# Row tails of a graph kernel stored in 28 parts, and three moves in the order of ScalarE, VectorE and TensorE

## The reference

```python
h  = relu(layernorm(x))
agg = segment_sum(relu(h[src]), dst)                       # layer 0
x1 = x + relu(relu((h + agg) @ W1 + b1) @ W2 + b2)
h  = relu(layernorm(x1))                                   # layer 1
deg_inv = where(deg > 0, deg ** -0.5, 0)                   # deg: edges per dst
norm = deg_inv[src] * deg_inv[dst] * edge_weight
Q, K, V = relu(h @ Wq + bq), h @ Wk + bk, h @ Wv + bv      # 8 heads of 8
hidden = V * hopwise[0]
hop 0:    Kj = relu(K[src] + edge_attr);  M = segment_sum(norm * outer(Kj, V[src]), dst)
hops 1,2: M = segment_sum(norm * M[src], dst)
each hop: H = Q . M;  hidden += hopwise[hop + 1] * H / max(1, |H| / sqrt(8))
out = x1 + hidden
```

## Time and profile before

| | us |
|---|---|
| median of 3 runs | 1816.73 (1809.44 to 1824.96) |
| profiled execution | 1815.59 |
| its span, first to last instruction | 1812.7 |
| DVE busy | 1488.8 (82%) |
| PE busy | 1345.3 (74%) |
| POOL busy | 1193.0 (66%) |
| ACT busy | 1015.2 (56%) |
| mean granted TensorE clock | 0.86 of full |

### The profile page before, as it was taken

How to read it: one execution, slowest core, us unless ns; L and a number is a source line. 1 busy time by engine, 2 the same in 40 slices (tenths; PEclk the granted TensorE clock), 3 DMA queues, 4 the chain that set the end, 5 groups by cost and what they waited for, 6 DMA issues and landing times. The chain is left out here.

```text
span 1812.7 us, 22165 instructions
## 1 busy us (share of the span) xinstructions
PE 1345.3 (74%) x5794; PEld 840.3 (46%) x5794; DVE 1488.8 (82%) x3207; ACT 1015.2 (56%) x2815; POOL 1193.0 (66%) x1185
## 2 busy tenths in 40 slices
PE   3666778788888985777777277778577898877772
PEld 3455666665666664454544033333233344455551
DVE  5866777789989886799999799999456788699992
ACT  4556878768878875455554255555355556333330
POOL 7775666616665531777773577777477777777776
PEclk9787898879978877798998589888799999988886
DMA  4394333334655554699998588888435554466650
GB/s 126 77 51 123 102 104 102 91 94 132 149 134 141 133 135 92 213 323 319 320 318 293 177 288 305 307 309 299 152 98 159 146 160 135 128 174 175 173 152 17
DMA packets 280787, 313.83 MB, mean 173 GB/s; under 512 B 168577, under 2 KB 198137, under 8 KB 268118
## 3 DMA queue, kind: packets, MB, share of 16 engines
q1 hardware_dynamic: 223734, 246.39, 45.3%
q0 software_dynamic: 56928, 66.04, 14.6%
HBM read 214.54 MB, written 161.32 MB: 207 GB/s over the span
## 5 line engine op out<-in xcount | busy, mean ns | idle before, releaser
L924 PE MATMUL bank<-product,ident 128*128 128x512 f32 (+1 forms) x800 | 383.3, 637 | 134.9 <-DVE product L1278 134.9
L533 POOL DMA_INDIRECT state<-state_hop,slot_of_src x392 | 395.6, 1009 | 126.1 <-issue 108.5
L703 ACT ACTIVATE bank<-state,norm 128x512 f32<-128x512 f32 x392 | 251.1, 679 | 254.9 <-DMA state<-state_hop,slot_of_src 221.6
L1278 DVE TENSOR_TENSOR product<-bank,queries 128x512 f32<-128x512 f32 x392 | 261.2, 687 | 90.0 <-ACT bank L703 88.3
L924 PEld LDWEIGHTS bank<-product,ident 128*128 128x128 f32 x800 | 160.9, 206 | 356.0 <-issue 182.7
L495 POOL DMA_INDIRECT x_edges<-in_x,dst_tiles x196 | 199.5, 1018 | 156.9 <-DVE x_edges L1188 97.0
L509 POOL DMA_INDIRECT row_of_src<-node_rows,pos_int x196 | 195.2, 996 | 122.2 <-DMA node_rows<-row_new 62.8
L495 POOL DMA_INDIRECT x_edges<-in_x,src_tiles x196 | 203.1, 1036 | 95.8 <-issue 54.4
L549 POOL DMA_INDIRECT out<-rows,dst_out x196 | 193.1, 985 | 59.7 <-issue 50.0
L831 PE MATMUL bank<-dst_steps,from_here 128*128 128x197 f32 x392 | 98.6, 406 | 101.7 <-ACT row_no L645 75.2
L1276 DVE SCALAR_TENSOR_TENSOR acc<-acc,same_as_before,bank 128x512 f32<-128x512 f32 x196 | 145.2, 741 | 15.9 <-ACT bank L703 15.1
(11 more groups left out here) (220 smaller groups left out, 3033.0 us busy)
## 6 DMA issues: line engine op xcount, KB each, us to landing
state_hop<-acc SPq DMA_DIRECT2D x98, 1024.0 KB, 4.7
x_nodes<-in_x SPq DMA_DIRECT2D x49, 256.0 KB, 3.6
src_row<-in_src_row SPq DMA_DIRECT2D x49, 256.0 KB, 3.6
out<-out_rows SPq DMA_DIRECT2D x49, 256.0 KB
dst_row<-in_dst_row SPq DMA_DIRECT2D x49, 256.0 KB, 4.5
kv_rows<-kv SPq DMA_DIRECT2D x49, 256.0 KB, 3.5
gg<-head_sums SPq DMA_DIRECT2D x98, 128.0 KB
kv_back<-kv_rows SPq DMA_DIRECT2D x49, 256.0 KB
```

What stands on the lines that cost most here:

```text
L533: pool.indirect_dma_start(out=mg[u % 4][:, k, :], out_offset=None, in_=d_m[hop - 1], in_offset=bass.IndirectOffsetOnAxis(ap=sidx[:, t:t + ...
L703: act.activation(pw[t % len(pw)][:, :], mg[u % 4][:, k, :], ACT.Copy, scale=wn12[:, t:t + 1]).then_inc(weighted, 1)
L924: ins = ten.matmul(ph[:, 0:k * D].rearrange("p (c j) -> p c j", j=HD), ident[:, :], part, start=(r == 0), stop=(r == HD - 1))
L1278: vec.tensor_tensor(ihj(pr[m % 2][:, u % 2 * EH + k, :]), ihj(pw[t % len(pw)][:, :]), over_j(Q[:, t, :]), ALU.mult).then_inc(multiplied, 1)
```

## The change

The store of the row tails is cut into 28 DMAs of 7 columns, at ticks 12 to 39, and POOL waits for all of them. On ACT, the root of the tick's statistics and the signs of the search move from behind the squares of x1 to ahead of the normalised rows, the root first; the signs take the search of group g-3 in place of g-2. On PE, the search moves behind the dense products. On DVE, x1 of the nodes (L1176) moves from the end of the tick to ahead of the statistics, the four comparisons of the selection become one instruction behind the statistics, and the computation of the slots from the signs comes a tick later.

```diff
@@ -61,6 +61,8 @@
 END = max(F_STEP)
 DENSE_TICKS = [2 * k for k in range(1, DU + 1)]
 assert len(DENSE_TICKS) == DU and all(t % 2 == 0 for t in DENSE_TICKS)
+TAIL = 7
+TAIL_AT = {12 + i: i * TAIL for i in range(T // TAIL)}
 DENSE_AT = {t: m for m, t in enumerate(DENSE_TICKS)}
 
 
@@ -405,9 +407,10 @@
                 u = g + 2 - S0
                 if 0 <= u < AU:
                     load_drow(u)
-                if g == 12:
+                if g in TAIL_AT:
+                    c = slice(TAIL_AT[g], TAIL_AT[g] + TAIL)
                     sync.wait_ge(tail_set, 2)
-                    sync.dma_start(by_slot(d_tab)[:, :, D:TW], tail[:, :, :]).then_inc(tail_kept, 16)
+                    sync.dma_start(by_slot(d_tab)[:, c, D:TW], tail[:, c, :]).then_inc(tail_kept, 16)
                 if g == B0 + 3:
                     sync.wait_ge(normed_e, AU)
                     for c in range(2):
@@ -498,7 +501,7 @@
                         bounds_check=top, oob_is_err=False).then_inc(edge_in[e % RI], 16)
 
             pool.wait_ge(pos_set, 1)
-            pool.wait_ge(tail_kept, 16)
+            pool.wait_ge(tail_kept, 16 * len(TAIL_AT))
             for b in range(3):
                 pool.wait_ge(t_kept[b], landed(AU - 1, b, 3))
             for u in range(CU):
@@ -599,6 +602,21 @@
                     act.wait_ge(ends_done, AU)
                     act.activation(flT[:, :], pfl[0:D, 0:2 * TILES], ACT.Copy).then_inc(ends_out, 1)
 
+                if g in STAT_NO:
+                    lo, hi = stats_at(g)
+                    act.wait_ge(varred, STAT_NO[g] + 1)
+                    act.activation(q[:, 3, lo:hi], q[:, 2, lo:hi], ACT.Sqrt, bias=epsc[:, 0:1],
+                                   scale=1.0 / (D * D)).then_inc(rooted, 1)
+                u = g - 3
+                if 0 <= u < CU:
+                    act.wait_ge(searched, u + 1)
+                    for k in range(EH):
+                        t = u * EH + k
+                        each = pair[:, 256 * k:256 * k + T]
+                        act.activation(each, each, ACT.Sign, bias=spm[:, t:t + 1],
+                                       scale=-1.0, accum_out=signs[:, t:t + 1])
+                    act.activation(rowno[:, u * EH:(u + 1) * EH],
+                                   pair[:, :].rearrange("p (k c) -> p k c", c=256)[:, :, T], ACT.Copy).then_inc(counted, 1)
                 if g - 1 in STAT_NO:
                     act.wait_ge(scaled, STAT_NO[g - 1] + 1)
                 u = g - 10 - B0
@@ -634,21 +652,6 @@
                     act.activation(flr[:, :, :], pfl[0:HALF, 0:4 * D].rearrange("p (k f) -> p k f", f=D),
                                    ACT.Copy).then_inc(ends_out, 1)
 
-                u = g - 2
-                if 0 <= u < CU:
-                    act.wait_ge(searched, u + 1)
-                    for k in range(EH):
-                        t = u * EH + k
-                        each = pair[:, 256 * k:256 * k + T]
-                        act.activation(each, each, ACT.Sign, bias=spm[:, t:t + 1],
-                                       scale=-1.0, accum_out=signs[:, t:t + 1])
-                    act.activation(rowno[:, u * EH:(u + 1) * EH],
-                                   pair[:, :].rearrange("p (k c) -> p k c", c=256)[:, :, T], ACT.Copy).then_inc(counted, 1)
-                if g in STAT_NO:
-                    lo, hi = stats_at(g)
-                    act.wait_ge(varred, STAT_NO[g] + 1)
-                    act.activation(q[:, 3, lo:hi], q[:, 2, lo:hi], ACT.Sqrt, bias=epsc[:, 0:1],
-                                   scale=1.0 / (D * D)).then_inc(rooted, 1)
                 if g == 7:
                     act.wait_ge(prep_v, 3)
                     act.activation(tmp2[:, :], tmp[:, :], ACT.Sqrt).then_inc(prep_a, 1)
@@ -823,14 +826,6 @@
                                 ins = ten.matmul(pfl[0:HALF, k * D:(k + 1) * D], lhs, flr[:, 2 * (1 - w) + i, :],
                                                  start=(i == 0), stop=(i == 1), skip_group_check=True)
                     ins.then_inc(fixes, 1)
-                u = g - 2
-                if 0 <= u < CU:
-                    ten.wait_ge(g_set, u + 1)
-                    wait(ten, counted, u)
-                    for k in range(EH):
-                        ins = ten.matmul(pair[:, 256 * k:256 * k + T + 1], gsel[u % 2][:, k * P:(k + 1) * P], delta[:, :],
-                                         start=True, stop=True, skip_group_check=True)
-                    ins.then_inc(searched, 1)
                 if g == B0 + 3:
 
                     ten.wait_ge(ends_out, 1)
@@ -856,6 +851,14 @@
                     ten.wait_ge(relued_d, m + 1)
                     wait(ten, x1_d, m)
                     rows_out(pbd, a1d, W2, 0, HT // 2, mm2_d)
+                u = g - 2
+                if 0 <= u < CU:
+                    ten.wait_ge(g_set, u + 1)
+                    wait(ten, counted, u)
+                    for k in range(EH):
+                        ins = ten.matmul(pair[:, 256 * k:256 * k + T + 1], gsel[u % 2][:, k * P:(k + 1) * P], delta[:, :],
+                                         start=True, stop=True, skip_group_check=True)
+                    ins.then_inc(searched, 1)
                 m = DENSE_AT.get(g - 6)
                 if m is not None:
                     ten.wait_ge(h1_d, m + 1)
@@ -1097,34 +1100,13 @@
 
             for g in range(END + 1):
                 qp, q = st[(g - 1) % RS], st[g % RS]
-                n_sel = 0
-
-                def select(n):
-
-                    nonlocal n_sel
-                    u = g - S0
-                    if 0 <= u < AU:
-                        if n_sel == 0:
-                            vec.wait_ge(drow_in[u % 3], landed(u, u % 3, 3))
-                            wait(vec, turned_e, u - 1)
-                        for k in range(n_sel, n_sel + n):
-                            t = u * EH + k
-                            ins = vec.tensor_scalar(sel[u % 2][:, k * P:(k + 1) * P], drow[u % 3][:, k * P:(k + 1) * P],
-                                                    tmf[:, t:t + 1], None, ALU.is_equal)
-                        n_sel += n
-                        if n_sel == EH:
-                            ins.then_inc(s_set, 1)
-
                 if g - 1 in STAT_NO:
                     lo, hi = stats_at(g - 1)
                     vec.wait_ge(rooted, STAT_NO[g - 1] + 1)
                     own.add(vec.reciprocal(qp[:, 4, lo:hi], qp[:, 3, lo:hi]))
-                    select(1)
                     own.sync()
                     vec.scalar_tensor_tensor(qp[:, 5, lo:hi], qp[:, 0, lo:hi], -1.0 / D, qp[:, 4, lo:hi],
                                              ALU.mult, ALU.mult).then_inc(scaled, 1)
-                else:
-                    select(1)
                 m = DENSE_AT.get(g - 1)
                 if m is not None:
                     vec.wait_ge(scaled, STAT_NO[g - 1] + 1)
@@ -1139,6 +1121,12 @@
                     own.add(vec.tensor_tensor(h1d[m % 2][:, :, :], x1d[m % RX][:, 0, :, :], each_row(qp[:, 4, 0:HT]), ALU.mult))
                     own.sync()
                     vec.tensor_tensor(h1d[m % 2][:, :, :], h1d[m % 2][:, :, :], each_row(qp[:, 5, 0:HT]), ALU.add).then_inc(h1_d, 1)
+                m = DENSE_AT.get(g - 4)
+                if m is not None:
+                    vec.wait_ge(mm2_d, m + 1)
+                    wait(vec, res_d, m - RX + 1)
+                    vec.scalar_tensor_tensor(flat(x1d[m % RX][:, 0, :, :]), pbd[:, :], 0.0, flat(xn[m % RX][:, 0, :, :]),
+                                             ALU.max, ALU.add).then_inc(x1_d, 1)
                 if g in STAT_NO:
                     lo, hi = stats_at(g)
                     m, m2, e, u = DENSE_AT.get(g), DENSE_AT.get(g - 5), g - 1, g - 9 - B0
@@ -1156,25 +1144,24 @@
                         own.add(vec.tensor_reduce(q[:, 0:2, HT:HT + EH], xe[e % RE][:, :, :, :], AX.X, ALU.add))
                     own.sync()
                     own.add(vec.tensor_tensor(q[:, 2, lo:hi], q[:, 0, lo:hi], q[:, 0, lo:hi], ALU.mult))
-                    select(1)
                     own.sync()
                     own.add(vec.scalar_tensor_tensor(q[:, 2, lo:hi], q[:, 1, lo:hi], float(D), q[:, 2, lo:hi],
                                                      ALU.mult, ALU.subtract))
-                    select(1)
                     own.sync()
                     vec.tensor_scalar(q[:, 2, lo:hi], q[:, 2, lo:hi], 0.0, None, ALU.max).then_inc(varred, 1)
-                    select(1)
+                u = g - S0
+                if 0 <= u < AU:
+                    vec.wait_ge(drow_in[u % 3], landed(u, u % 3, 3))
+                    wait(vec, turned_e, u - 1)
+                    vec.tensor_tensor(sel[u % 2][:, :].rearrange("p (k c) -> p k c", c=P),
+                                      drow[u % 3][:, :].rearrange("p (k c) -> p k c", c=P),
+                                      tmf[:, u * EH:(u + 1) * EH].unsqueeze(2).to_broadcast([P, EH, P]),
```

(9 more changed lines are left out.)

## The result

The changed kernel takes 1878.53 us (median of 4 runs, 1873.29 to 1882.21), the kernel before 1818.92 on the same chip. The ratio is 1.033, with a 95% interval of 1.0278 to 1.0383: slower, and outside the range that I gave. The profiled execution's span is 1870.6 us against 1812.7, so 57.9 us are to be explained.

The account below looks back on a forecast made before the run. No engine was full; a chain back and forth between engines set each front tick. The terms -17.9 - 3.7 + 3.4 - 2.0 + 6.6 + 8.3 - 1 + 1 = -5.3 took 1815.59 to 1810.3, stated as 1811 us; range 1784 to 1842.

Parts of the forecast that it names:

- Part 1: Tail store in 28 parts, ticks 12 to 39: parts hidden, the whole 17.9 us stall on DVE comes back.
- Rival (d): The parts of the tail store stall as the one did, 0.64 us each: 1828 us in all; chance 0.09.
- Parts 2 and 3: New ACT-DVE loop: 6.29 a tick in ticks 10 to 50, gain 3.7 us; 6.59 in 58 to 98, gain 2.0.
- Part 4: Start, ticks 2 to 10: preparation waits for PE's search, reciprocal for a late root; +8.3 us, bounds 0 and 10.
- Part 5: Early x1 waits for PE at the low clock: +6.6 us in ticks 58 to 98, +3.4 in 10 to 50.
- rival (c): x1 waits for PE at the low clock more often; ten and twelve waits give 1850 us; chance 0.18.
- Rival (a): Start and clock cost nothing, as PE's smaller gaps keep the clock high: 1792 us; chance 0.21.

Follow-up runs that it names:

- the copies first: The changed kernel with ACT's two edge copies (L640, L645) ahead of the normalised rows; ratio 1.0007 to the kernel before.
- the parts alone: The kernel before with the tail store in 28 parts, nothing else; 2060.76 us, ratio 0.9873.
- the last kernel: The kernel before with the tail store in 28 parts and the four comparisons merged into one behind the statistics; 1810.6 us, ratio 0.992.

## Why the prediction was wrong

**Part 1 was right.** The stall is gone, parts are hidden, and the kernel before with parts and one comparison has the 17.9 us less in ticks 10 to 50. Rival (d) is refuted: no wait for a source row or an output row stands out in ticks 12 to 39. The rule of the Trainium skill, "DMA: Bandwidth & Descriptors", section "Rules for kernel authors", would have them joined. The runs here disagree: the single store costs 17.9 us in ticks 10 to 50 in the order of before and 14.9 in the new one, so the measurement decides against joining for this store, which nobody waits for in the front and behind which others queue.

**Parts 2 and 3 were right for a PE at full clock.** I had loops of 6.29 and 6.59 and stretches of 251.6 and 263.6; with PE's gaps filled they are 253.1 and 267.5. The difference in the second is the even tick's 6.8 in place of 6.6. The merged comparison, taken at 0.3, costs 0.13 in the old order.

**Part 4 was right.** +8.3 foreseen, 10.2 measured, both waits at their places (5.2 and 3.8 after V, foreseen 5.0 and 3.7), and 6.6 to 9.4 come back when their causes are moved.

**Part 5 failed**, in size and number, in the step "ACT is free 4.6 after V of the even tick, copy 0.6, PE's two groups 2.9" and "the groups start at about 6.6 and end 5.2 after V: 2.2 late". The late x1 was the right mechanism, rival (c)'s. But I followed only the dense groups' own inputs. PE works its queue in order, and at its head stands the edge product L771 that waits for L645; the new order on ACT puts root and eight rows ahead of that copy. So PE's whole tick starts 3.9 after V and not 1.9, and the groups end 7.1 after V(69) at the low clock, 4.2 late instead of 2.2. The terms of my own part 3 had it: 0.21 + 0.21 + 1.32 + 1.59 is 3.33 to the start of L645, and with its 0.46 it is 3.8. And the wait itself makes the gaps (up to 2.8 us) that I had put at 1.1 in this stretch, from which I took three late ticks. There were twelve. 311.8 less 267.5 is 44.3 us for the clock in 58 to 98, where I took 6.6, and 271.9 less 253.1 is 18.8 in 10 to 50, where I took 3.4. These two sizes, 37.7 and 15.4 above what I took, are 53.1 of the 63.2 us between my sum of -5.3 and the 57.9 measured. The rest are 1.9 of the start, 1.5 and 3.9 of the two loops, -0.8 and 2.0 of the ticks 50 to 58 and 98 on, and 1.6 behind the front.

In ticks 10 to 50 the failed step is the count: two late ticks, taken because the gaps would shrink to about 2.4. They shrank to 2.5, and ten ticks were late all the same. About 14 of the 18.8 us also come back, with nothing filled, when the search stands behind the transposes; I had put the transposes' delay at the low clock at 0.6 a time, and in the forecast at nothing.

Rival (a) had the clock stay high with the more even loop: the reverse happened. In ticks 58 to 98 the more even loop of the other engines raised PE's idle time at the head of its ticks from 32.5 to 55.2 us. Rival (c) had the right wait, but its cap was ten waits of 2.2 in ticks 58 to 98, where there were twelve late ticks that cost about 3.7 each, and 1850 was not far enough. Its threshold was summed wrongly too: from -5.3, three waits of 2.2 more make the kernel slower than before and eleven by 1%, not seven and thirteen. What could have been read beforehand is in the waits of before, 410 to 676 us:

```profile
PE bank L768 <- DVE x_edges L1188: 32.5, 20, 2.4
```

An edge step already made PE wait twenty times here, up to 2.4 us, and with x1 at the end of DVE's tick DVE did not wait for the product. The question which instruction opens PE's tick, and where its input stands on ACT in the new order, would have given the 3.9.

The Trainium skill, "TensorE: Matmul & The Clock Gate", section "A second HAM failure mode: psum-queue depth-cycling", says that a TensorE which idles briefly but often between groups of products can swing between its two levels. The trace agrees: the mean clock is 0.80 with gaps of up to 2.8 us in each pair of ticks, and 0.99 with the same order and the gaps filled.

The 1.6 us behind the front are within the scatter: the code there is the same in every kernel, and from V(106) on it took 1103.5 to 1112.3 us in the eight profiles on the other two chips. What stays open is why ticks 58 to 98 alternate between stretches of 6.8 and of 10.6 at the same order of work, and why ten ticks in 10 to 50 are late though the gaps shrank: the runs show that filling them or moving the search takes most of it away, not what sets the count.

## What to carry to other kernels

When a step is moved ahead on one engine, list what it pushes back, and for each of those ask which other engine has it at the head of its queue: the whole queue behind starts late, not just the one product. An engine whose clock depends on its own work, as TensorE's did here, should be priced at the low clock wherever the new order opens a regular gap in it, and a step that needs its result has most slack at the end of the waiting engine's tick. Where the gaps cannot go, shorter ones may do: the copies first left PE as much idle time as before them, at a mean clock of 0.98. A cheap test of the clock: fill the gap with idle work; if the kernel gets faster, it was the clock.

## What the hardware showed that I had not expected

- Adding work made the kernel faster: two idle products of 512 columns in each odd tick, some 32 us of PE in all (240.3 us busy against 208.1 with the copies first), took ticks 58 to 98 from 311.8 to 269.4 us.
- TensorE idled 2.8, 0.8, 2.4, 0.8 and 2.4 us ahead of five ticks in a row, and the granted clock went from 1.00 (459 to 490 us) to 0.50 (491 to 499 us); with the longest gap of the filled kernel at 1.6 the mean stayed at 0.99, and with the copies first, 59.2 us of idle time in gaps of at most 1.8, at 0.98.
- The kernel before took 1818.92 us beside the changed one, 1824.03 and 1827.69 on two chips and 2082.09 on a third. On that chip the parts alone took 268.3 us in ticks 58 to 98, where the last kernel took 271.0; but 97.6 against 54.9 from V(2) to V(10), and 1317.7 against 1105.6 from V(106) on.
